# An attention-plus-experts block on one core: the list that orders every engine's work is planned anew

## The chip, the cores and the metric

The kernel runs on one core of a Trainium2 chip. The metric is the device time of one execution in microseconds (us), median of several runs; lower is better. Times below are counted from the start of the profiled span.

## The reference, cut to what matters

Two sequences of 2048 tokens with 128 features are normalised, then go through causal attention and through a layer of 8 experts; the results are added. Each token goes to the one expert whose centroid matches it best.

```python
def block(x, qk, ov, centroids, ln_g, ln_b, w1, b1, w2, b2):      # x: (2, 2048, 128)
    xn = layernorm(x)
    scores = einsum('bsd,de,bte->bst', xn, qk, xn) / sqrt(128)     # causal mask, softmax
    attn = einsum('bst,btd,de->bse', softmax(scores), xn, ov)
    eid = argmax(xn @ centroids.T)                                 # one of 8 experts
    alpha = sigmoid(sum(xn * centroids[eid]))
    xln = layernorm(xn) * ln_g[eid] + ln_b[eid]
    ffn = relu(xln @ w1[eid] + b1[eid]) @ w2[eid] + b2[eid]        # 128 -> 512 -> 128
    return x + attn + xn + alpha * ffn
```

## The kernel before

All five engines are programmed by hand, with semaphores between them. One list, ORDER (line 68), holds 1120 entries such as `T.3` or `P.17`. Every engine walks the whole list once, in its own program, and emits the instructions that it has for each entry. So the list alone fixes the order on each engine; where an entry stands against the entries of another engine has no meaning by itself. The waits are in the code of the entries. An engine executes in order: an instruction that waits holds up all that stands behind it on that engine.

The work has these stages. The 32 tiles of 128 tokens are in 8 groups of 4.

- **Normalising.** VAR (VectorE, statistics), LE (ScalarE, root), RN (GpSimd, one refining step on small columns), ROW (VectorE, line 799, groups 0, 1, 4, 6) or XA (ScalarE, line 1067, groups 2, 3, 5, 7).
- **Keys, queries, values, expert weights.** T, Q, V and W1 on TensorE; the entries with a, f or h (Ta, Qa, Vf, Va, W1h) copy the high half of a result out on ScalarE, those with l (Tl, Ql, Vl, W1l) the low half on VectorE, or on GpSimd for Vl.0, Vl.1 (line 741) and all W2l (line 735).
- **A first pass over the scores** for the row maxima: M (TensorE, line 1277), MR (VectorE, lines 892 and 896), RM, SH, SHa.
- **Attention** in 80 steps: X (scores, lines 1300 to 1304), EH and EX (exponential on ScalarE, lines 1044 and 1050), XL (VectorE, line 910, low half, from step 12), P and PB (weighted sums, lines 1334, 1343, 1344, 1351), QT (VectorE, lines 923 and 927, quotients).
- **Second normalising and routing.** R2 and R2n (VectorE) with R2a (ScalarE) make the second root; BASE and S (GpSimd, lines 641 and 651) add to and scale the rows; CH.0 and CH.1 (VectorE, lines 818 to 834) choose the expert of each half of the tokens; CNT (TensorE) and PL (VectorE, lines 849 to 860) work out each token's place; Sh and Sl make the two halves of a scaled row (Sl at line 1014); SIG makes the gate.
- **Sends.** 32 entries SC (GpSimd, line 684), one per tile, scatter the rows to an expert-sorted array in HBM, with a memset of 600 elements after each (line 671) to space them. SC.0 needs PL. Then SyncE reads the sorted rows back, transposed (line 526).
- **Experts.** 39 tiles: HI (TensorE, lines 1434 to 1436), RE (ScalarE, line 1166), LO (VectorE, line 1018), OUT (TensorE, lines 1456 to 1462), YS (ScalarE, line 1174), SO (GpSimd, line 693, scatter back). HI.0 needs all sends, since SyncE waits for them.
- **The rest of the attention** (steps 52 to 79) follows behind the experts on TensorE, then Y adds the experts' rows, and the results are stored.

GpSimd works in this order: the constants, RN, BASE, W2l, S, Vl.0 and Vl.1, then the 32 SC, W2l.5 to W2l.7, then the 39 SO. The part of CH that the prediction speaks of is three operations with both inputs in SBUF and four reductions:

```python
v.tensor_reduce(aff[:, on, :], parts, AX.X, ALU.add).then_inc(s_aff, 1)
v.wait_ge(s_aff, h + 1)
v.tensor_reduce(amax[:, on], aff[:, on, :], AX.X, ALU.max).then_inc(s_choose, 1)
v.wait_ge(s_choose, n + 1)
v.tensor_tensor(hit[:, on, :], aff[:, on, :], amax[:, on].unsqueeze(2).broadcast_to(wide),
                ALU.is_equal).then_inc(s_choose, 1)
```

Of the kernel before, what the change touches and what calls it, by code (L numbers as in the profile page):

```python
# [69 lines left out]
Vl.0 RN.3.4 BASE.2 RN.4.6 T.1 AE.1 AE.2 C1a LE.1.2 C2a Ta.0 W1h.0 W1h.1 Ta.1 W1l.0 Qa.0 Vf.0 LE.2.3 AE.3 W1l.1 AE.4  # L70
W1h.2 Va.0 Qa.1 LE.3.4 W1l.2 LE.4.6 XA.2 Vf.1 Ta.2 C2v C1v Tl.0 ROW.1.2 VAR.2.3 BASE.3 RN.6.8 W2l.0 W2l.1 BASE.4 BASE.5
BASE.6 BASE.7 W2l.2 Z.0 W2l.3 COL0 S.0 S.1 S.2 S.3 S.4 VAR.3.4 Tl.1 Ql.0 VAR.4.6 MR.0.0.0.0 Ql.1 MR.0.0.3.0 W1b.0 Q.0
V.0 W1.2 Z.1 Z.2 W1b.1 M.0.0.0.0 Q.1 MR.0.0.2.0 MR.0.0.1.0 VAR.6.8 RM.0.0 Tl.2 MR.0.1.1.0 M.0.0.3.0 S.5 S.6 W2l.4 W1.3
Z.3 S.7 W1b.2 M.0.0.1.0 M.0.0.2.0 V.1 T.2 M.0.1.1.0 W1.4 M.0.1.3.1 M.0.1.0.1 MR.0.1.3.1 MR.0.1.0.1 M.0.1.1.1 W1b.3
M.0.1.2.1 Q.2 M.0.1.3.0 MR.0.1.1.1 W1h.3 XA.3 LE.6.8 W1l.3 M.0.1.2.0 MR.0.1.2.1 MR.0.1.3.0 Ql.2 MR.0.1.2.0 SH.0.0
ROW.4.6 R2 ROW.6.8 MR.0.1.0.0 RM.0.1 MR.0.2.3.1 MR.0.2.1.1 MR.0.2.1.0 W1l.4 MR.0.2.3.2 MR.0.2.2.1 W1l.5 Qa.2 XA.5
SHa.0.0 AE.5 W2.0 W2.1 W1h.4 W1h.5 XA.7 EX.0 SHa.0.1 EX.1 W2.2 W2.3 M.0.2.3.1 M.0.2.1.1 M.0.1.0.0 W1.5 X.0 MR.0.2.2.0
R2a EX.2 EX.3 EX.4 Ta.3 Ta.4 Ta.5 W2.4 Ta.6 EX.5 Ta.7 Sh.0 Qa.3 EX.6 X.1 M.0.2.1.0 X.2 M.0.2.3.2 SH.0.1 M.0.2.2.1
M.0.2.1.2 X.3 M.0.2.2.0 M.0.2.0.1 P.0 M.0.2.0.0 X.4 M.0.2.0.2 MR.0.2.1.2 MR.0.2.0.1 M.0.2.3.0 P.1 T.3 T.4 T.5 X.5 P.2
T.6 P.3 T.7 X.6 M.0.2.2.2 MR.0.2.0.0 MR.0.2.0.2 MR.0.2.3.0 R2n Q.3 Tl.3 Tl.4 QT.0.0.0 Tl.5 Tl.6 QT.0.0.1 Tl.7  # L80
MR.0.2.2.2 Ql.3 RM.0.2 X.7 P.4 M.0.3.1.0 MR.0.3.1.0 M.0.3.3.1 MR.0.3.3.1 MR.0.3.2.0 M.0.3.2.0 X.8 AFF.0 AFFr.0.1
AFFr.0.2 M.0.3.1.1 X.9 AFFr.0.3 AFF.1 AFFr.1.1 X.10 P.5 MR.0.3.1.1 CH.0 Vl.1 MR.0.3.0.3 CH.1 Sl.0 SIG PL AFFr.1.2
M.0.3.0.3 P.6 AFFr.1.3 SH.0.2 M.0.3.3.2 X.11 V.2 P.7 CNT P.8 X.12 P.9 X.13 P.10 MR.0.3.3.2 Vl.2 QT.0.1.0 QT.0.1.1
# [25 lines left out]
YS.12 RE.29 RE.30 YS.13 RE.31 RE.32 YS.14 RE.33 YS.15 RE.34 RE.35 RE.36 YS.16 RE.37 XL.50 XL.51 QT.1.1.0 QT.1.1.1 LO.0
LO.1 M.1.3.3.0 X.51 PB.47 P.49 PB.48 P.50 PB.49 P.51 HI.0 PB.50 PB.51 HI.1 HI.2 OUT.0 LO.2 MR.1.3.1.0 MR.1.3.1.3 LO.3  # L110
OUT.1 HI.3 HI.4 OUT.2 HI.5 M.1.3.0.2 OUT.3 HI.6 OUT.4 HI.7 OUT.5 HI.8 OUT.6 LO.4 LO.5 LO.6 LO.7 LO.8 MR.1.3.0.2 LO.9
LO.10 LO.11 M.1.3.0.0 HI.9 OUT.7 HI.10 OUT.8 HI.11 OUT.9 HI.12 OUT.10 HI.13 OUT.11 HI.14 OUT.12 HI.15 OUT.13 HI.16
OUT.14 HI.17 LO.12 MR.1.3.3.0 LO.13 MR.1.3.0.0 LO.14 LO.15 LO.16 LO.17 MR.1.3.3.2 LO.18 MR.1.3.3.3 LO.19 LO.20 LO.21
LO.22 MR.1.3.0.3 LO.23 LO.24 LO.25 LO.26 LO.27 MR.1.3.1.2 LO.28 MR.1.3.2.0 LO.29 MR.1.3.2.1 LO.30 LO.31 LO.32
MR.1.3.2.2 LO.33 LO.34 OUT.15 M.1.3.3.2 HI.18 OUT.16 M.1.3.3.3 HI.19 OUT.17 M.1.3.0.3 SH.1.2 HI.20 OUT.18 HI.21 OUT.19
HI.22 OUT.20 HI.23 OUT.21 HI.24 OUT.22 HI.25 OUT.23 M.1.3.1.2 HI.26 M.1.3.2.1 OUT.24 HI.27 OUT.25 HI.28 M.1.3.2.0
OUT.26 HI.29 OUT.27 HI.30 OUT.28 M.1.3.2.2 HI.31 OUT.29 HI.32 OUT.30 M.1.3.2.3 HI.33 OUT.31 HI.34 OUT.32 MR.1.3.1.1
LO.35 LO.36 MR.1.3.3.1 LO.37 MR.1.3.2.3 LO.38 RM.1.3 XL.52 XL.53 HI.35 M.1.3.1.1 OUT.33 M.1.3.3.1 HI.36 OUT.34 HI.37
OUT.35 HI.38 OUT.36 X.52 OUT.37 X.53 X.54 P.52 X.55 PB.52 P.53 X.56 PB.53 P.54 X.57 PB.54 P.55 P.56 X.58 PB.55 SH.1.3
PB.56 X.59 P.57 PB.57 X.60 OUT.38 P.58 PB.58 P.59 X.61 X.62 PB.59 P.60 X.63 PB.60 X.64 P.61 P.62 PB.61 X.65 PB.62 P.63  # L120
X.66 P.64 X.67 PB.63 XL.54 XL.55 XL.56 XL.57 XL.58 XL.59 XL.60 XL.61 XL.62 XL.63 XL.64 XL.65 XL.66 XL.67 Y.6 XL.68 Y.0
XL.69 Y.7 XL.70 XL.71 Y.3 Y.2 Y.1 XL.72 Y.5 Y.4 XL.73 XL.74 QT.1.2.0 XL.75 XL.76 QT.1.2.1 XL.77 XL.78 XL.79 RE.38 EH.52
EX.52 YS.17 EH.53 EX.53 EH.54 EX.54 YS.18 EH.55 EX.55 EH.56 EX.56 EH.57 EX.57 EH.58 EX.58 EH.59 EX.59 SHa.1.3 EH.60
# [1372 lines left out]
```

## Time and profile before

| | us |
|---|---|
| three runs | 223.23, 223.56, 226.32 |
| their median | 223.56 |
| span of the profiled execution | 223.1 |
| TensorE busy in the span | 206.3 (92%) |
| VectorE busy | 175.5 (79%) |
| ScalarE busy | 155.2 (70%) |
| GpSimd busy | 154.3 (69%) |

The profile gives no time of its own for the profiled execution beside the span; the span lies 0.13 us below the fastest of the three runs and 0.46 us below their median. Reductions by 1 us are 0.45%. Engines in the rows: PE is TensorE, DVE is VectorE, ACT is ScalarE, POOL is GpSimd, SP is SyncE; L799 is line 799 of the kernel.

### The profile page before, as it was taken

The numbers are of one execution on the slowest core, as the hardware profiler recorded it, in microseconds if no ns is written. First come the engines' busy times: TensorE is split into PE (matmuls) and PEld (weight loads), VectorE is DVE, ScalarE is ACT, GpSimd is POOL, SyncE is SP. The second block draws the span as 40 slices with busy tenths as digits, with TensorE's granted clock in tenths as the row PEclk, the third lists the DMA queues.
The fourth block names the chain that finished last, engine by engine and source line by source line (L and its number), as shares of the span: only waits on it lengthen the run. The fifth ranks groups of instructions, "written<-read, shape, count | busy, mean of one in ns | idle before, by whom it ended". The sixth has DMA issues, their size and how long they took to land.

```text
span 223.1 us, 6878 instructions
## 1 busy us (share of the span) xinstructions
PE 206.3 (92%) x2428; PEld 159.9 (72%) x2428; DVE 175.5 (79%) x448; ACT 155.2 (70%) x346; POOL 154.3 (69%) x230
## 2 busy tenths in 40 slices
...
GB/s 167 314 289 64 6 0 94 116 355 232 5 12 39 36 39 39 44 43 40 36 40 36 128 198 160 125 92 141 131 150 92 50 40 37 38 35 172 256 193 141
DMA packets 37601, 23.55 MB, mean 106 GB/s; under 512 B 12472, under 2 KB 34144, under 8 KB 37568
## 3 DMA queue, kind: packets, MB, share of 16 engines
q1 hardware_dynamic: 34960, 18.28, 32.3%
...
q10 hardware_dynamic: 336, 0.14, 0.3%
q14 instruction: 13, 0.11, 0.2%
...
## 4 chain that ended last, share of the span: by engine, by line
PE 77%; DVE 11%; ACT 4%; issue 4%; DMA 2%; SPq 1%; DVEq 0%; ACTq 0%
PE psum L1343 6%; PE psum L1300 6%; PE psum L1301 6%; PE psum L1302 6%; PE psum L1351 6%; PE psum L1344 6%; PE psum L1277 5%; PE psum L1460 4%; PE psum L1461 4%; PE psum L1462 4%; PE psum L1434 4%; PE psum L1436 4%; PE psum L1435 4%; PE psum L1260 3%; PE psum L1334 2%
## 5 line engine op out<-in xcount | busy, mean ns | idle before, releaser
L910 DVE TENSOR_TENSOR p_lo<-p_sb,p_hi 128x512 f16<-128x512 f32 (+1 forms) x68 | 42.0, 638 | 12.2 <-ACT p_sb L1050 12.0
L1044 ACT ACTIVATE p_hi<-psum 128x512 f16<-128x512 f32 (+1 forms) x68 | 37.1, 547 | 19.4 <-PE psum L1351 14.2
L1050 ACT ACTIVATE p_sb<-psum 128x512 f32<-128x512 f32 (+1 forms) x80 | 42.5, 539 | 6.8 <-PE psum L1334 6.7
L693 POOL DMA_INDIRECT sorted_y<-xn x39 | 38.1, 977 | 11.6 <-ACT xn L1174 5.5
L1018 DVE SCALAR_TENSOR_TENSOR h_lo<-psum,h_hi 128x512 f16<-128x512 f32 x39 | 26.8, 690 | 21.5 <-ACT h_hi L1166 18.7
L671 POOL MEMSET v_full<- 1x600 f32 x71 | 41.7, 588 | 0.0
L684 POOL DMA_INDIRECT sorted_x<-xr,pos x32 | 33.5, 1047 | 11.9 <-issue 11.4
L1166 ACT ACTIVATE h_hi<-psum 128x512 f16<-128x512 f32 x39 | 23.3, 597 | 21.0 <-PE psum L1436 19.2
L1343 PE MATMUL psum<-v_hi,p_hi 128*128 128x129 f16 x236 | 32.7, 220 | 1.2 <-DVE x_sb L927 1.2
L896 DVE TENSOR_REDUCE row_max<-psum 128x1 f32<-128x512 f32 x48 | 32.3, 682 | 1.6 <-PE psum L1277 1.1
L1344 PE MATMUL psum<-v_lo,p_hi 128*128 128x128 f16 x236 | 32.6, 219 | 0.0
L1277 PE MATMUL psum<-kT_hi,qT_hi 128*128 128x512 f16 (+3 forms) x80 | 26.3, 349 | 4.5 <-DVE row_max L896 1.8
L1434 PE MATMUL psum<-x2T,w_hl 128*128 128x128 f16 x156 | 28.0, 219 | 0.2 <-issue 0.2
L1460 PE MATMUL psum<-w_hl,h_hi 128*128 x156 | 28.1, 219 | 0.0
L1461 PE MATMUL psum<-w_hl,h_hi 128*128 x156 | 28.1, 219 | 0.0
L1462 PE MATMUL psum<-w_hl,h_lo 128*128 x156 | 28.1, 219 | 0.0
L1436 PE MATMUL psum<-x2T,w_hl 128*128 128x128 f16 x156 | 28.0, 219 | 0.0
L1435 PE MATMUL psum<-x2T,w_hl 128*128 128x128 f16 x156 | 28.0, 219 | 0.0
L1300 PE MATMUL psum<-qT_hi,kT_hi 128*128 128x512 f16 (+1 forms) x80 | 27.8, 347 | 0.0
L1302 PE MATMUL psum<-qT_hi,kT_lo 128*128 128x512 f16 (+1 forms) x80 | 27.8, 347 | 0.0
L1301 PE MATMUL psum<-qT_lo,kT_hi 128*128 128x512 f16 (+1 forms) x80 | 27.8, 347 | 0.0
L1343 PEld LDWEIGHTS psum<-v_hi,p_hi 128*128 128x128 f16 x236 | 23.0, 98 | 4.1 <-DVE x_sb L927 1.3
...
## 6 DMA issues: line engine op xcount, KB each, us to landing
...
sorted_y<-xn POOLq DMA_INDIRECT x39
sorted_x<-xr,pos POOLq DMA_INDIRECT x32
```

Of the source, the lines that this page charges most:

```text
L671: pool.memset(idle, 0.0).then_inc(s_idle, 1)
L693: pool.indirect_dma_start(out=sorted_y[:, :], out_offset=bass.IndirectOffsetOnAxis(ap=tokens, axis=0), in_=xs[:, t % SLOTS, 0:P], in_offse ...
L910: v.tensor_tensor(p_lo[:, u, off:GW], p_sb[:, u, off:GW], p_hi[:, u, off:GW], ALU.subtract).then_inc(s_plo, 1)
L1044: a.activation(p_hi[:, u, off:GW], bank[SCORE[n % R]][:, off:GW], ACT.Exp, scale=SCALE).then_inc(s_exph, 1)
L1050: a.activation(p_sb[:, u, off:GW], bank[SCORE[n % R]][:, off:GW], ACT.Exp, scale=SCALE).then_inc(s_exp, 1)
L1277: mm(at[:, 0:w], qT_hi[:, q:q + P], kT_hi[:, k:k + w], start=True, stop=True).then_inc(s_mm, 1)
L1300: mm(at[:, off:GW], kT_hi[:, kk], qT_hi[:, q], start=True, stop=False)
L1301: mm(at[:, off:GW], kT_hi[:, kk], qT_lo[:, q], start=False, stop=False)
L1302: m = mm(at[:, off:GW], kT_lo[:, kk], qT_hi[:, q], start=False, stop=not diag)
L1343: mm(to[i], w, v_hi[:, kt, 0:P + 1], start=(j == 0 and i % 2 == 0), stop=False, skip_group_check=True)
L1344: mm(to[i][:, 0:P], w, v_lo[:, kt, :], start=False, stop=False, skip_group_check=True)
L1460: mm(to, h_hi[:, h, at], hi, start=False, stop=False, skip_group_check=True)
```

## The change

Only the text of ORDER differs: the same 1120 entries in another sequence, planned with durations of a trace. No instruction, buffer or wait rule is changed. Some of the list's 60 lines; the first shows how the start differs, the others how the sends (SC) are now spread among other engines' entries:

```diff
-VAR.0.1 VAR.1.2 BIASa LE.0.1 C0a AE.0 WU C0 C1 C2 T.0 W1.0 W1.1 BIAS RN.0.1 ROW.0.1 RN.1.2 MISC BASE.0 BASE.1 RN.2.3
...
-QT.0.2.1 MR.1.0.2.0 XL.25 Ql.5 RM.1.0 MR.1.1.1.0 Ql.6 XL.26 MR.1.1.2.0 MR.1.1.0.1 SC.0 SC.1 SC.2 SC.3 SC.4 SC.5 SC.6
...
+VAR.0.1 WU VAR.1.2 LE.0.1 C0 BIASa RN.0.1 ROW.0.1 C0a BIAS C1 C2v C1a C1v Tl.0 LE.1.2 C2a C2 T.0 W1.0 ROW.1.2 AE.0 Ta.0
...
+S.7 V.2 EX.14 MR.0.3.3.1 XL.13 P.11 PICK SC.0 EH.15 X.13 Sh.2 XL.14 MR.0.3.1.1 X.14 X.15 M.0.3.0.0 M.0.3.3.1 EX.15 X.16
...
```

On GpSimd, here is the stretch from the constants to the first send, as a piece of the difference (- before, + now). L735 is W2l, L641 is BASE, L651 is S, L741 is Vl.1, L684 the first SC.

```order
 L755 TENSOR_TENSOR x_sb<-x_sb,col 128x32
-L651 TENSOR_TENSOR xn<-xn,r 128x4x127 x7
+L641 TENSOR_TENSOR x_sb<-x_sb,xn 128x4x127
+L735 TENSOR_TENSOR w_hl<-w_raw,w_hl 128x512
+L651 TENSOR_TENSOR xn<-xn,r 128x4x127 x2
 L735 TENSOR_TENSOR w_hl<-w_raw,w_hl 128x512
 L651 TENSOR_TENSOR xn<-xn,r 128x4x127
+L641 TENSOR_TENSOR x_sb<-x_sb,xn 128x4x127
...
 L741 TENSOR_TENSOR v_lo<-v_full,v_hi 128x512
+L651 TENSOR_TENSOR xn<-xn,r 128x4x127 x3
 L684 DMA sorted_x<-xr,pos 4992x130
```

Before, seven S stood together, then W2l.4, the eighth S and Vl.1. Now the S are mixed with three W2l and one BASE, and Vl.1 stands ahead of the last three; in all S.0, S.1, W2l.2, S.2, BASE.7, S.3, W2l.3, S.4, W2l.4, Vl.1, S.5, S.6, S.7.

On VectorE, this is what stands ahead of CH.0 and in it, before. L896 is MR, L818 begins CH.0.

```order
L971 SCALAR_TENSOR_TENSOR qT_lo<-psum,qT_hi 128x512
L904 TENSOR_REDUCE max_col<-row_max 128x4
L896 TENSOR_REDUCE row_max<-psum 128x1 x4
L818 TENSOR_REDUCE aff<-psum 128x128
L820 TENSOR_REDUCE amax<-aff 128x16
L822 TENSOR_TENSOR hit<-aff,amax 128x128
```

And now, from the same L904 to the end of CH.0 and on to what follows CH.1:

```order
L904 TENSOR_REDUCE max_col<-row_max 128x4
L896 TENSOR_REDUCE row_max<-psum 128x1
L818 TENSOR_REDUCE aff<-psum 128x128
L820 TENSOR_REDUCE amax<-aff 128x16
L822 TENSOR_TENSOR hit<-aff,amax 128x128
...
L834 TENSOR_REDUCE onehot_group<-onehot 128x32
L872 TENSOR_SCALAR eneg<-eneg 128x32
```

Three MR have moved from ahead of CH.0 to behind it, and SIG (L872) stands directly behind CH.1, ahead of one MR and Sl.0.

## Rows read from the trace of the kernel before

**Rows 1.** The page: busy shares, and the group of MR (busy us, mean ns).

```profile
PE 206.3 (92%) x2428; PEld 159.9 (72%) x2428; DVE 175.5 (79%) x448; ACT 155.2 (70%) x346; POOL 154.3 (69%) x230
...
L896 DVE TENSOR_REDUCE row_max<-psum 128x1 f32<-128x512 f32 x48 | 32.3, 682 | 1.6 <-PE psum L1277 1.1
```

**Rows 2.** Busy time of each engine in four stretches.

```profile
core 0: us, PE busy (x) PEld busy (x) DVE busy (x) ACT busy (x) POOL busy (x), PEclk, DMA share, GB/s
0.00:30.00 30.00, 24.13 (x108) 13.03 (x108) 23.61 (x112) 19.27 (x53) 16.71 (x60) 0.89 0.56 156
30.00:62.70 32.70, 28.55 (x264) 20.88 (x265) 30.21 (x84) 24.50 (x54) 21.10 (x26) 1.00 0.41 137
62.70:126.20 63.50, 61.83 (x669) 44.43 (x667) 60.82 (x142) 49.19 (x104) 54.41 (x66) 1.00 0.14 42
126.20:219.70 93.50, 91.83 (x1390) 81.55 (x1390) 59.77 (x109) 62.23 (x138) 62.04 (x79) 1.00 0.52 123
```

**Rows 3.** Sends, transposed loads, experts, last matmul (start us, us, engine, line, operation).

```profile
63.67 1.21 POOL L684 DMA_INDIRECT sorted_x<-xr,pos  x1 [6.63 <-issue]
...
121.93 1.31 SPq L526 DMA_TRANSPOSE x2T<-sorted_x  x1
...
126.19 0.23 PE L1434 MATMUL psum<-x2T,w_hl 128*128 128x128 f16 x1 [0.21 <-issue]
...
219.45 0.23 PE L1351 MATMUL psum<-v_hi,p_lo 128*128 128x129 f16 x1
```

**Rows 4.** VectorE's waits: line, waited for, us in total, times, longest.

```profile
DVE b_hl L960 <- ACT b_hi L1096: 1.3, 1, 1.3
...
DVE G_lo L953 <- ACT cent_hl L1091: 1.0, 1, 1.0
```

**Rows 5.** VectorE and GpSimd, single instructions where both read SBUF; first one alone.

```profile
31.32 0.34 DVE L799 TENSOR_SCALAR xn<-x_sb,mv,r 128x127 f32<-128x127 f32 x1
...
12.78 1.51 DVE L799 TENSOR_SCALAR xn<-x_sb,mv,r 128x127 f32<-128x127 f32 x1
...
13.03 1.16 POOL L641 TENSOR_TENSOR x_sb<-x_sb,xn 128x508 f32<-128x508 f32 x1
...
33.43 1.26 DVE L799 TENSOR_SCALAR xn<-x_sb,mv,r 128x127 f32<-128x127 f32 x1
...
121.85 2.04 DVE L910 TENSOR_TENSOR p_lo<-p_sb,p_hi 128x512 f16<-128x512 f32 x1
...
121.08 1.15 POOL L735 TENSOR_TENSOR w_hl<-w_raw,w_hl 128x512 f16<-128x512 f32 x1
...
122.19 1.15 POOL L735 TENSOR_TENSOR w_hl<-w_raw,w_hl 128x512 f16<-128x512 f32 x1
```

**Rows 6.** GpSimd, scaling of the rows (S): first, two in the middle, last.

```profile
43.80 1.04 POOL L651 TENSOR_TENSOR xn<-xn,r 128x508 f32<-128x508 f32 x1 [0.35 <-DVE r L771]
...
48.78 2.03 POOL L651 TENSOR_TENSOR xn<-xn,r 128x508 f32<-128x508 f32 x2
...
51.88 1.03 POOL L651 TENSOR_TENSOR xn<-xn,r 128x508 f32<-128x508 f32 x1
```

**Rows 7.** VectorE: CH.0 (three), CH.1 (one), Sl.0, PL's first and last instruction.

```profile
52.92 0.42 DVE L818 TENSOR_REDUCE aff<-psum 128x128 f32<-128x256 f32 x1
...
53.70 0.29 DVE L822 TENSOR_TENSOR hit<-aff,amax 128x128 f32<-128x128 f32 x1
...
55.00 0.38 DVE L834 TENSOR_REDUCE onehot_group<-onehot 128x32 f16<-128x128 f16 x1
...
56.84 0.35 DVE L822 TENSOR_TENSOR hit<-aff,amax 128x128 f32<-128x128 f32 x1
...
58.49 0.68 DVE L1014 TENSOR_TENSOR xr<-xn,xr 128x512 f16<-128x512 f32 x1
...
59.77 0.16 DVE L849 TENSOR_SCALAR tiles_f<-psum 128x8 f32<-128x8 f32 x1
...
62.47 0.18 DVE L860 CAST pos<-posf 128x32 uint32<-128x32 f32 x1
```

More of the change, by code:

```diff
@@ L68 @@
 ORDER = entries("""
-VAR.0.1 VAR.1.2 BIASa LE.0.1 C0a AE.0 WU C0 C1 C2 T.0 W1.0 W1.1 BIAS RN.0.1 ROW.0.1 RN.1.2 MISC BASE.0 BASE.1 RN.2.3
[L70 to L83, printed above, removed]
@@ L109 @@
[L109 to L123, printed above, removed]
@@ new lines @@
+M.0.1.1.0 Vf.1 Z.0 W1.4 Ta.2 Tl.2 MR.0.1.2.1 MR.0.1.1.0 W1l.2 RN.4.6 LE.4.6 M.0.1.3.1 AE.5 MR.0.1.3.1 MR.0.1.0.0 W1h.3
+LE.6.8 W2.0 W1b.3 M.0.1.0.0 MR.0.1.2.0 MR.0.1.3.0 M.0.1.2.0 W1l.3 RN.6.8 MISC ROW.4.6 M.0.1.3.0 SH.0.0 W1l.4 W2l.0
+W1h.4 MR.0.1.1.1 BASE.3 W1.5 MR.0.1.0.1 R2 SHa.0.0 Ql.2 M.0.1.1.1 Q.2 M.0.1.0.1 W2.1 X.0 BASE.4 X.1 ROW.6.8 Qa.2 BASE.5
+RM.0.1 W1h.5 W1l.5 M.0.2.3.2 M.0.2.1.1 X.2 M.0.2.1.0 X.3 P.0 MR.0.2.3.2 M.0.2.2.0 COL0 MR.0.2.1.1 MR.0.2.1.0 MR.0.2.2.0
+EX.0 XA.3 MR.0.2.2.1 BASE.6 M.0.2.2.1 EX.1 MR.0.2.3.1 P.1 XA.5 M.0.2.3.1 SH.0.1 W2l.1 S.0 M.0.2.0.1 M.0.2.0.0
@@ new lines @@
+MR.0.2.0.1 XA.7 M.0.2.1.2 S.1 SHa.0.1 R2a X.4 W2l.2 MR.0.2.0.0 EX.2 W2.2 Ta.3 Ta.4 P.2 MR.0.2.1.2 S.2 R2n EX.3
+M.0.2.0.2 T.3 MR.0.2.0.2 T.4 QT.0.0.0 Tl.3 BASE.7 Tl.4 T.5 Tl.5 Ta.5 X.5 X.6 M.0.2.3.0 EX.4 S.3 P.3 EX.5 MR.0.2.3.0 T.6
+QT.0.0.1 Z.1 Ta.6 T.7 Tl.6 Ta.7 Q.3 Qa.3 X.7 EX.6 W2.3 M.0.2.2.2 Tl.7 Ql.3 P.4 M.0.3.1.0 W2.4 MR.0.2.2.2 Sh.0 AFF.0
+AFFr.0.1 AFFr.0.2 AFFr.0.3 W2l.3 EX.7 X.8 AFF.1 S.4 Va.1 AFFr.1.1 RM.0.2 EX.8 SGa EX.9 MR.0.3.1.0 W2l.4 CH.0 CH.1 Vl.1
+SIG EX.10 AFFr.1.2 SHa.0.2 AFFr.1.3 SH.0.2 M.0.3.2.0 P.5 MR.0.3.2.0 X.9 S.5 EH.12 P.6 Sl.0 X.10 EX.11 P.7 EX.12 S.6
@@ new lines @@
+X.11 CNT PL QT.0.1.0 MR.0.3.0.1 QT.0.1.1 P.8 XL.12 Vl.2 P.9 Va.2 X.12 EH.13 EX.13 M.0.3.0.1 P.10 EH.14 MR.0.3.0.0 Sh.1
+S.7 V.2 EX.14 MR.0.3.3.1 XL.13 P.11 PICK SC.0 EH.15 X.13 Sh.2 XL.14 MR.0.3.1.1 X.14 X.15 M.0.3.0.0 M.0.3.3.1 EX.15 X.16
+SC.1 P.12 EH.16 Sl.1 MR.0.3.3.2 EX.16 EH.17 M.0.3.1.1 PB.12 EX.17 P.13 M.0.3.3.2 Sh.3 M.0.3.0.2 P.14 EH.18 XL.15 P.15
+PB.13 SC.2 SC.3 X.17 EX.18 X.18 MR.0.3.0.2 EH.19 Va.3 M.0.3.1.3 MR.0.3.1.3 PB.14 P.16 X.19 SC.4 SC.5 XL.16 M.0.3.0.3
+MR.0.3.0.3 SC.6 PB.15 M.0.3.2.3 M.0.3.3.3 MR.0.3.2.3 XL.17 SC.7 X.20 MR.0.3.3.3 EX.19 M.0.3.3.0 PB.16 MR.0.3.3.0 V.3
```

75 lines of the change are left out of this document (45 added, 30 removed).

## The prediction

> **What bounds the kernel now.** I read the busy shares first. TensorE works for 206.3 of 223.1 us [rows 1]: no instruction goes away, so only its 16.8 us of idle time can be won. The table by stretches says where that lies [rows 2]. From 126.2 to 219.7 us TensorE is busy for 91.83 of 93.5 us, and from 62.7 to 126.2 for 61.83 of 63.5; after 219.7 come 3.4 us of quotients and stores. The idle time is in the first 62.7 us, where TensorE works for 52.7 us. Its clock is 0.89 of full there in the first 30 us and 1.00, that is 2.4 GHz, from then on.
>
> What TensorE waits for in that stretch is VectorE: from 30 to 62.7 us it is busy for 30.21 of 32.7 us. It works 23.61 + 30.21 = 53.8 us up to the end of PL, so 8.9 us are idle, 6.4 of them in the first 30 [rows 2]. Two of its waits can be named: 1.3 us in BIAS (L960) and 1.0 us at line 953 [rows 4].
>
> The end of PL sets what follows. PL ends at 62.47 + 0.18 = 62.65 us [rows 7], the first send starts 1.02 us later, at 63.67, the transposed loads can begin at 121.93, and the first expert matmul runs at 126.19 [rows 3]. From the first send that is 62.5 us. It is a chain of 32 sends and idle-memsets on GpSimd, none of which the change shortens. Beside it VectorE is busy for 60.82 and TensorE for 61.83 of 63.5 us [rows 2], so all three are close to full, and the start of the experts can't move by more than PL moves. From the first expert matmul to the end of the span 223.1 - 126.2 = 96.9 us pass, nearly all TensorE's own work. So what PL gains or loses is what the kernel gains or loses.
>
> **The change, part by part.** *Work ahead of PL.* The durations are those of the trace, taken along the new order. Three MR (MR.0.3.3.1, MR.0.3.1.1, MR.0.3.0.3) fall behind PL. Two are whole ones, 32.3 / 48 = 0.67 us by the group [rows 1]; less the small overlap of neighbours and with the short third, they are some 1.4 us. They aren't saved: they come later, in a stretch that VectorE doesn't bound alone.
>
> *Two holds go.* Line 799 takes 0.34 us when GpSimd is quiet, but 1.51 us at 12.78, when BASE.0 runs from 13.03 to 14.19, and 1.26 us at 33.43, beside a W2l [rows 5]. It ends with GpSimd's instruction: 1.17 + 0.92 = 2.1 us lost. In the new order BASE.0 stands behind a second RN, and the last ROW falls where GpSimd waits for XA.3, so I count both as gone. If they meet again, 2.1 us come back.
>
> *Idle time.* BIAS waits for a load and stands behind RN.0.1 and ROW.0.1 now: its 1.3 us are covered by them. Of the other waits I take 1.5 us as gone, since C1a goes ahead of the A_e copies on ScalarE and the first T, Q and XA are out about a microsecond sooner. The 1.0 us at line 953 stays, since C2a depends on the same chain as before. So 8.9 - 2.8 = 6.1 us remain. The bounds are 3.0 (the start, the first load and line 953 alone) and 8.9 (nothing won).
>
> *PL without anything new:* 53.8 - 1.4 - 2.1 + 6.1 = 56.4 us, with bounds of 53.3 and 59.2. That is 6.3 us sooner than 62.65, and would be the gain of the kernel.
>
> *The new collision.* I don't expect to see this gain, and the reason lies in the order on GpSimd. Before, S.0 starts at 43.80, right behind R2n; S runs at 2.03 / 2 = 1.0 us a piece, and S.7 ends at 51.88 + 1.03 = 52.91 [rows 6]. CH.0 starts at 52.92 [rows 7]: they just miss each other. Now R2n comes sooner by 0.6 us (less work ahead), 2.1 us (the holds) and 2.0 us (idle time): S.0 starts at 39.1. But three W2l, one BASE and Vl.1 are mixed in, at 1.15 us or so each [rows 5], about 1.12 by their pitch: the run takes 8 x 1.0 + 5 x 1.12 = 13.6 us and ends at 52.7. CH.0 comes in the midst of it. Backward from PL at 56.4: PL is 62.65 - 59.77 = 2.88, Sl.0 and SIG 59.77 - 58.49 = 1.28, one MR 0.6, CH.0 55.38 - 52.92 = 2.46, and CH.1 the same [rows 7]. So CH.0 starts at 46.7, and its first operation with two inputs in SBUF (L822, 53.70 - 52.92 = 0.78 us later) at 47.5, 5.2 us before the run ends.
>
> What does such an operation do there? The third case in the rows tells most: line 910 is asked for at 121.85, while W2l.5 runs (121.08 to 122.23). It takes 2.04 us, to 123.89, which is 0.55 us behind the end of W2l.6 (122.19 + 1.15 = 123.34) [rows 5]. A row of that size takes 0.68 us alone, as Sl.0 shows [rows 7]. So it was let in neither when W2l.5 ended nor while W2l.6 ran: the two followed one another without a gap. If a run of two holds VectorE to its end, I expect a run without gaps to do so too. For L822 itself the trace shows next to nothing: 0.35 instead of 0.29 us at 56.84, beside the last 0.2 us of Vl.1 [rows 7]. Its cost has the bounds 0 and 5.2 us; I take 5.2, by the nearest row.
>
> *Sum.* L822 ends at 52.7 + 0.3, the rest of CH.0 takes 1.4, CH.1 2.5, Sl.0 and SIG 1.3, the MR 0.6, PL 2.9: PL ends at 61.7, against 62.65. TensorE stands at CNT meanwhile, with all attention steps behind it, but catches up: after it the sends set the pace. Result: 223.1 - 0.95 = 222.15, say 222.2 us. This goes by the span of 223.1; the median of the runs is 223.56.
>
> *After the sends.* The same matmuls in another mixture. I set them at nothing: TensorE is full, and the attention left over covers the last OUT. At the very end step 79's scores come closer to their PB; a few tenths.
>
> The Trainium skill (SBUF — State Buffer, "Who interferes with whom") says that a VectorE instruction with two SBUF inputs contends with a GpSimd instruction that reads SBUF, and that whoever issues first has the shared ports for the whole instruction. The holds at 12.78 and 33.43 agree with that. Read to the letter, each hold would end with one GpSimd instruction; the row at 121.85 shows a hold over two. What the letter would give here is the second rival.
>
> **The rivals.**
> 1. *No hold for these operations.* CH works on 128 x 128 elements, a quarter of what line 910 reads, and the trace shows no long hold of one; or ScalarE is late for W2l.3 or Vl.1, and the gap lets CH through. Then PL ends at 56.4 and the kernel takes 223.1 - 6.25 = 216.9 us. Against it: line 799 is as small (127 columns) and was held twice.
> 2. *One hold, one GpSimd instruction.* The six operations of CH would each wait for one instruction of the run: the first to 48.2, then 49.3, 50.4; behind the reductions of both halves 52, 52.7, and the last is free. CH.1 ends at 54.0 instead of 51.6, PL at 58.8: 223.1 - 3.85 = 219.2 us.
> 3. *Slower: the experts stall.* By the order, the TensorE work between HI.k and OUT.k falls below 2.5 us for 15 of 39 tiles, instead of 3 (12 matmuls an HI, 13 an OUT, at some 0.055 us). In between, RE on ScalarE and LO on VectorE must be done. If a tile needs 2.5 us, because a YS or an MR gets ahead, and the 12 added tiles each lose 0.4 us, 4.8 us are lost where TensorE is the bound: with the forecast's PL, 222.2 + 4.8 = 227.0 us. It decides from 1 us of such stalls on, which eats up what PL gains. Against it: TensorE lost only 93.5 - 91.8 = 1.7 us there before [rows 2].
>
> **How the numbers follow.** Forecast (held to the end of the run) 0.55, own range 221.0 to 224.0; rival 1 0.20; rival 2 0.14; rival 3 0.11. The range reaches into rival 1 and towards rival 3: 216.8 to 225.0. About 2% is what a measurement of this kernel can tell, so faster means below 219.1 and slower above 228.0: faster takes rival 1 and most of half of rival 2 and a little of the forecast, 0.20 + 0.07 + 0.02 = 0.29; slower is the far part of rival 3, 0.04; the rest, 0.67, is within 2%.
>
> **What would show it.** In the changed profile: S.0 near 39 and S.7 ending near 52.7; L822 of CH.0 with a duration of several us, ending with S.7; PL's end at 61 to 62; the first send 1 us later; the first expert matmul 62 us behind it; 92 to 94 us of TensorE from there. L822 at 0.3 us near 47.5 makes the forecast wrong, and rival 1 right; six operations of about 1 us each speak for rival 2; a first send at 63 and an end beyond 224 with waits ahead of line 1456 for rival 3. If the holds at line 799 are still there, or S.0 starts after 42, my walk of the first 40 us failed.

## The result, and the profile after

| | before | after |
|---|---|---|
| median of 20 runs each, us | 224.25 | 222.31 |
| lowest and highest | 222.11 to 226.32 | 221.39 to 224.81 |
| span of the profiled execution | 223.1 | 220.4 |
| end of PL | 62.65 | 59.48 |
| first send | 63.67 | 60.51 |
| first expert matmul | 126.19 | 123.09 |
| end of the last matmul | 219.68 | 217.11 |

The ratio is 0.9938 with an interval of 0.9916 to 0.9960: 0.6% or 1.4 us faster, less than the 2% that counts as a change. (It is less than the 1.9 us between the medians because it leaves out four executions that took over 1.5% more than the fastest of their kernel.) The two profiled executions differ by more, 2.7 us. The changed kernel's profiled execution took 222.19 us for a span of 220.4, so some 1.8 us lie around a span. The forecast of 222.2 took the span of before (223.1) for its time, and is therefore a forecast of a span.

The busy shares of the changed kernel, and the granted clock in 40 slices of the span:

```profile
PE 203.7 (92%) x2428; PEld 159.9 (73%) x2428; DVE 178.0 (81%) x448; ACT 154.4 (70%) x346; POOL 156.0 (71%) x230
...
PEclk9999997999999999999999999999999999999999
```

TensorE's busy time fell by 2.6 us [rows 1] though its instructions are the same. The table by stretches (its columns as in [rows 2]), cut at the milestones of this execution, says where:

```profile
0.00:30.00 30.00, 24.01 (x127) 13.04 (x128) 27.04 (x124) 23.31 (x61) 17.71 (x64) 1.00 0.70 201
30.00:59.50 29.50, 25.03 (x244) 20.32 (x243) 27.15 (x68) 18.00 (x42) 20.35 (x21) 0.94 0.32 106
59.50:123.10 63.60, 62.23 (x671) 44.71 (x671) 62.11 (x143) 50.68 (x108) 53.95 (x66) 1.00 0.14 42
123.10:217.10 94.00, 92.46 (x1392) 81.79 (x1391) 60.65 (x111) 62.42 (x138) 63.97 (x79) 1.00 0.53 119
...
30.00:32.00 2.00, 0.97 (x10) 0.64 (x8) 2.00 (x5) 2.00 (x7) 1.73 (x2) 1.00 0.44 126
32.00:37.00 5.00, 4.54 (x22) 3.67 (x22) 3.75 (x8) 1.82 (x6) 4.79 (x7) 0.66 0.00 0
```

Two things are to be seen. In the first 30 us the clock is now whole, where it was 0.89 [rows 2]; it falls to the lower level, 1.2 GHz, between 32 and 37 instead, after a stretch in which TensorE was busy for 0.97 of 2 us. And VectorE does 27.0 us of work in the first 30 instead of 23.6, which is the gain of the front. Not all of it is the order's. e3_mixture below has the order of before on every engine up to R2, but ran at a mean clock of 0.991 instead of 0.985, and it reaches R2 (its first line here) 1.6 us sooner (the first row is the kernel before, the second e3_mixture):

```profile
32.34 0.18 DVE L804 TENSOR_TENSOR ve<-r 128x32 f32<-128x32 f32 x1
...
30.75 0.19 DVE L808 TENSOR_TENSOR ve<-r 128x32 f32<-128x32 f32 x1
```

So about half of the 3.2 us by which PL came sooner goes with the longer stretch at the lower clock in the profiled execution of before, and not with the order. Behind PL the two kernels take the same time, 63.6 and 94.0 us instead of 63.5 and 93.5 [rows 2].

TensorE's idle time up to its last matmul is 217.11 - 203.75 = 13.4 us, and it was 219.68 - 206.33 = 13.4 before. So between these two executions TensorE gained nothing in waits, and 2.6 us in the time of its matmuls. The clock accounts for some 1.6 us of that, by an estimate: a mean of 0.985 over 223.1 us against 0.992 over 220.4, of which the missing shares are 3.4 and 1.8 us. What makes the rest isn't shown. Its waits are others now:

```profile
engine line waited for: us in total, times, longest us
PE psum L1239 <- DVE onehot_group L834: 2.6, 1, 2.6
...
PE psum L1351 <- DVE p_lo L910: 1.3, 2, 1.1
```

L1239 is CNT, which needs the last operation of CH.1; the second row is PB.47, which needs XL.47. Neither wait stands in the list of before. The first has its cause here, in GpSimd's run (line by line) and VectorE's CH:

```profile
39.45 1.04 POOL L651 TENSOR_TENSOR xn<-xn,r 128x508 f32<-128x508 f32 x1 [2.44 <-DVE r L771]
...
47.19 1.04 POOL L651 TENSOR_TENSOR xn<-xn,r 128x508 f32<-128x508 f32 x1
48.19 1.21 POOL L735 TENSOR_TENSOR w_hl<-w_raw,w_hl 128x512 f16<-128x512 f32 x1
49.36 1.16 POOL L741 TENSOR_TENSOR v_lo<-v_full,v_hi 128x512 f16<-128x512 f32 x1
50.48 3.12 POOL L651 TENSOR_TENSOR xn<-xn,r 128x508 f32<-128x508 f32 x3
...
47.50 0.88 DVE L822 TENSOR_TENSOR hit<-aff,amax 128x128 f32<-128x128 f32 x1
48.41 1.13 DVE L825 TENSOR_TENSOR hit<-hit,rank_w 128x128 f32<-128x128 f32 x1
49.58 0.29 DVE L828 TENSOR_REDUCE posf<-hit 128x16 f32<-128x128 f32 x1
49.90 0.78 DVE L830 TENSOR_TENSOR onehot<-hit,posf 128x128 f16<-128x128 f32 x1
...
51.77 0.94 DVE L822 TENSOR_TENSOR hit<-aff,amax 128x128 f32<-128x128 f32 x1
52.75 1.01 DVE L825 TENSOR_TENSOR hit<-hit,rank_w 128x128 f32<-128x128 f32 x1
...
59.30 0.18 DVE L860 CAST pos<-posf 128x32 uint32<-128x32 f32 x1
```

S.0 starts at 39.45 and L822 at 47.50, as forecast (39.1 and 47.5), and the run ends at 53.60. But L822 takes 0.88 us and not 5.5: it ends 0.15 us behind the S that ran when it was asked for (47.19 + 1.04 = 48.23). L825 ends as far behind W2l.4, L830 behind Vl.1, and so on. Five of the six operations wait for one GpSimd instruction each, 0.6 + 0.8 + 0.5 + 0.65 + 0.7 = 3.3 us over their 0.29 [rows 7]; the reductions (L828) aren't held.

The second wait:

```profile
115.79 1.11 POOL L684 DMA_INDIRECT sorted_x<-xr,pos  x1 [0.17 <-issue]
116.89 0.59 POOL L671 MEMSET v_full<- 1x600 f32 x1
117.46 2.26 POOL L735 TENSOR_TENSOR w_hl<-w_raw,w_hl 128x512 f16<-128x512 f32 x2
...
116.66 3.61 DVE L910 TENSOR_TENSOR p_lo<-p_sb,p_hi 128x512 f16<-128x512 f32 x1
...
120.33 0.40 PE L1351 MATMUL psum<-v_hi,p_lo 128*128 128x129 f16 x4 [1.13 <-DVE p_lo L910]
```

XL.47 is asked for 0.24 us before the last send ends and finishes at 120.27, 0.55 us behind the second W2l. It is the operation that took 2.04 us before [rows 5], and here it is held through the end of the send, a memset and two W2l. So there are holds of two kinds, and the forecast had taken its size from the wrong one.

### The profile page after: what moved, and what is told of

Its sections match the earlier page's. It is cut to its first block, busy times and chain, and to the rows that moved or that the text cites. A ratio compares the mean times of both kernels' runs of the same rounds, so it can differ in the third digit from the quotient of the medians.

```text
span 220.4 us, 6878 instructions
## 1 busy us (share of the span) xinstructions
PE 203.7 (92%) x2428; PEld 159.9 (73%) x2428; DVE 178.0 (81%) x448; ACT 154.4 (70%) x346; POOL 156.0 (71%) x230
## 4 chain that ended last, share of the span: by engine, by line
PE 47%; DVE 14%; POOL 11%; DMA 6%; issue 5%; SPq 1%; ACT 0%; DVEq 0%; POOLq 0%
POOL sorted_y L693 7%; PE psum L1277 4%; POOL v_full L671 4%; DVE p_lo L910 4%; PE psum L1351 3%; PE psum L1343 3%; PE psum L1344 3%; PE psum L1301 3%; PE psum L1300 3%; PE psum L1302 3%; PE psum L1434 3%; DMA sorted_y<-xn 3%; PE psum L1436 3%; PE psum L1435 3%; DMA xn<-sorted_y 3%
## 5 line engine op out<-in xcount | busy, mean ns | idle before, releaser
L910 DVE TENSOR_TENSOR p_lo<-p_sb,p_hi 128x512 f16<-128x512 f32 (+1 forms) x68 | 43.7, 658 | 10.9 <-ACT p_sb L1050 10.7
L693 POOL DMA_INDIRECT sorted_y<-xn x39 | 40.0, 1026 | 10.7 <-issue 5.3
L1018 DVE SCALAR_TENSOR_TENSOR h_lo<-psum,h_hi 128x512 f16<-128x512 f32 x39 | 26.8, 690 | 21.8 <-ACT h_hi L1166 19.7
L684 POOL DMA_INDIRECT sorted_x<-xr,pos x32 | 33.0, 1033 | 12.2 <-ACT v_hi L1122 6.9
L896 DVE TENSOR_REDUCE row_max<-psum 128x1 f32<-128x512 f32 x48 | 32.0, 683 | 1.4 <-PE psum L1277 1.3
L1344 PEld LDWEIGHTS psum<-v_lo,p_hi 128*128 128x128 f16 x236 | 23.1, 98 | 3.1
```

What stands on the lines that cost most here:

```text
L693: pool.indirect_dma_start(out=sorted_y[:, :], out_offset=bass.IndirectOffsetOnAxis(ap=tokens, axis=0), in_=xs[:, t % SLOTS, 0:P], in_offse ...
L910: v.tensor_tensor(p_lo[:, u, off:GW], p_sb[:, u, off:GW], p_hi[:, u, off:GW], ALU.subtract).then_inc(s_plo, 1)
L1344: mm(to[i][:, 0:P], w, v_lo[:, kt, :], start=False, stop=False, skip_group_check=True)
```

## The experiments

Theory A: an operation of VectorE with two inputs in SBUF waits for one GpSimd instruction, CH's waits move the end of PL and TensorE's CNT, and these set the end. Theory B: the hold lasts to the end of a run without gaps (the forecast). Theory C: PL's date doesn't decide. The ratios are to the kernel before, run on the same chip; the changed kernel has 0.9938 (0.9916 to 0.9960).

**e4_ports: the hold by itself.** A program of its own:

```diff
+    ("WWWWW", ("red", "E512")),
+    ("SSSSS", ("red", "CH")),
...
+                    ins = pool.tensor_tensor(out=w2_hl[:, i + 1, :], in0=w2_raw[:], in1=w2_hl[:, 0, :], op=ALU.subtract)
```

> No attention and no experts: the input is copied to the output, and runs of 2 to 6 GpSimd operations without gaps (W: 128x512 f32 and f16 to f16, S: 128x508 f32 scaled in place) are set against single VectorE operations of 128, 256 and 512 columns, asked for some 0.7 us into the run. Theory A: each VectorE operation ends 0.1 to 0.55 us behind the end of the GpSimd instruction that ran when it was asked for, whatever its size. Theory B: each ends behind the last instruction of the run. A third outcome, by which both rows of the traces so far would hold: those of 128 columns are let in at the next boundary, and those of 512 columns only at the end of the run.

One case with W and one with S, and the same form alone (L92 is W, L95 is S, L116 the form of XL, L118 that of L822):

```profile
9.80 0.29 DVE L118 TENSOR_TENSOR hit<-aff,amax 128x128 f32<-128x128 f32 x1
...
10.79 6.04 POOL L92 TENSOR_TENSOR w_hl<-w_raw,w_hl 128x512 f16<-128x512 f32 x5
11.46 1.02 DVE L116 TENSOR_TENSOR p_lo<-p_sb,p_hi 128x512 f16<-128x512 f32 x1
...
48.63 5.06 POOL L95 TENSOR_TENSOR xn<-xn,r 128x508 f32<-128x508 f32 x5
49.29 0.53 DVE L118 TENSOR_TENSOR hit<-aff,amax 128x128 f32<-128x128 f32 x1
```

The W run goes on to 16.83, but XL's form is through at 12.48; in the S run L822's is through at 49.82. All sizes and mixtures did so: theory A, and the size of the operation is not what holds XL.47. GpSimd's next instruction is held in turn: the run of five W takes 6.04 us against 5.59 in the case with the smallest hold. Each case stands twice in the program, and the second time agrees within 0.02 us.

**e11_ports2: what precedes the run.** The same program with indirect stores and memsets ahead of the W.

```diff
+    ("WW", R + ("E512",)),
+    ("mWW", R + ("E512",)),
+    ("DmWW", R + ("E512",)),
+    ("DmWWWW", R + ("E512", "E512")),
```

> No attention and no experts: the input is copied to the output. An indirect store (D), a memset of 600 elements (m) and 2 or 4 operations of the form of W2l (W) follow one another on GpSimd; VectorE asks for an operation of the form of XL while D, m or the first W runs. Theory A alone: it is let in at once beside D and m, and behind the first W otherwise. If a preceding indirect store or memset makes the hold last over all W that follow, as at XL.47 in the kernels, it ends 0.55 us behind the last W in those cases, and in the case without D and m behind the first.

Three of the cases (L111 is W, L107 the memset, L100 the store, L137 XL's form):

```profile
13.68 0.59 POOL L107 MEMSET idle<- 1x600 f32 x1
14.24 2.25 POOL L111 TENSOR_TENSOR w_hl<-w_raw,w_hl 128x512 f16<-128x512 f32 x2
14.37 2.68 DVE L137 TENSOR_TENSOR p_lo<-p_sb,p_hi 128x512 f16<-128x512 f32 x1
...
21.47 1.11 POOL L100 DMA_INDIRECT sorted_x<-rows_out,pos  x1 [0.68 <-POOL tick L92]
21.55 0.69 DVE L137 TENSOR_TENSOR p_lo<-p_sb,p_hi 128x512 f16<-128x512 f32 x1
...
36.63 6.45 DVE L137 TENSOR_TENSOR p_lo<-p_sb,p_hi 128x512 f16<-128x512 f32 x2
37.49 0.59 POOL L107 MEMSET idle<- 1x600 f32 x1
38.06 4.47 POOL L111 TENSOR_TENSOR w_hl<-w_raw,w_hl 128x512 f16<-128x512 f32 x4
```

Two W alone let it in after the first (11.53 to 12.55), as in e4_ports; there GpSimd waits for the end of the short memset that opens the case. Two W directly behind a memset hold it to 17.05, 0.56 us behind the second; four W hold the second of two operations to 43.08, 0.55 behind the fourth. Beside the store it runs in 0.69, but asked for in the store's last 0.2 us, as XL.47 is, it is held through the memset and both W (26.94 to 30.54). So the rows of both kinds were right, and the long hold belongs to runs that follow a memset for whose end GpSimd doesn't wait, which is what W2l.5 and W2l.6 do behind the last send. The run of CH has no memset ahead of it. Why a memset does that, the runs don't tell.

The Trainium skill (SBUF — State Buffer, "Who interferes with whom") gives the ports to whoever issues first, for the whole instruction. CH in the changed kernel and e4_ports agree with that (0.88 and 0.53 us, each to some 0.15 us behind one instruction); e11_ports2 doesn't, with 2.68 us over two.

**e3_mixture: GpSimd's part of the change alone.** All other engines follow the list of before.

```diff
+            mixed = entries("S.0 S.1 W2l.2 S.2 BASE.7 S.3 W2l.3 S.4 W2l.4 Vl.1 S.5 S.6 S.7")
```

> The list of before, with GpSimd alone taking S.0 to S.7 in the mixture of the change (W2l.2, BASE.7, W2l.3, W2l.4 and Vl.1 among them); all else as before. The run then lasts from about 42 or 43.8 to 57, and CH.0 and CH.1 fall into it. Theory A: the operations with two inputs in SBUF take 0.8 to 1.1 us each instead of 0.3, CH.0 and CH.1 together 2.6 to 3.2 us more, PL ends at 65.2 to 65.8, the span is 225.7 to 226.3. Theory B: one operation takes 3.7 us, PL ends at 66.4, the span is 226.8. Theory C: span 223.

Median 224.86, ratio 1.0046 (1.0017 to 1.0075): 1.0 us slower, less than expected. CH.1 and Sl.0 in it (L829 is L825 of before, L1018 is Sl.0):

```profile
55.65 1.01 DVE L829 TENSOR_TENSOR hit<-hit,rank_w 128x128 f32<-128x128 f32 x1
...
58.03 1.12 DVE L1018 TENSOR_TENSOR xr<-xn,xr 128x512 f16<-128x512 f32 x1
```

Vl.1 waited 2.7 us for ScalarE, so GpSimd stood still beside CH.0, which was free. The holds sum to 1.6 us, against 2.6 to 3.2 expected; each is of kind A. PL ends at 62.63, as in the profile of before, only because this execution came to CH.0 sooner: from CH.0's start to the end of PL it takes 11.3 us (51.34 to 62.63) instead of 9.7 [rows 7]. So the change's mixture alone costs time.

**e1_order and e2_no_hold: the price of a hold.** Both move work out of GpSimd's run; e2_no_hold differs only in W2l.3 and W2l.4, which are memsets there, so it leaves out work.

```diff
-W2l.0 BASE.3 BASE.4 BASE.5 COL0 BASE.6 W2l.1 S.0 S.1 W2l.2 S.2 BASE.7 S.3 W2l.3 S.4 W2l.4 Vl.1 S.5 S.6 S.7
+W2l.0 W2l.1 BASE.3 BASE.4 BASE.5 COL0 BASE.6 W2l.2 BASE.7 Vl.1 S.0 S.1 S.2 S.3 S.4 S.5 S.6 S.7 W2l.3 W2l.4
```

> The changed list, with W2l.1, W2l.2, BASE.7 and Vl.1 moved ahead of S.0 on GpSimd (ScalarE's W2.2 and Va.1 earlier for that), S.0 to S.7 in one piece, W2l.3 and W2l.4 behind S.7, the clearing of rows Z.1 to Z.3 earlier. Theory A (each operation of CH waits for one GpSimd instruction, and the end of PL sets the end): S.7 ends at 47.8, two operations of CH.0 are held, by W2l.3 and W2l.4, CH.1 is free; PL ends at 57.7 instead of 59.5, the span is 218.6 instead of 220.4. Theory B (held to the end of a run without gaps): the first held operation goes to 50.1, PL ends at 57.9, nearly the same; the operations' own durations tell A from B. Theory C (the end of PL doesn't set the end): PL earlier, span still 220.4.

> As the run e1_order, but W2l.3 and W2l.4 are memsets: the low halves of w2 of experts 3 and 4 are left out (set to zero). Nothing on GpSimd reads SBUF against CH.0 and CH.1 any more but the last 0.3 us of S.7. Theory A and B: CH.0 and CH.1 take 2.5 us each, PL ends at 56.5, the first send is at 57.5, the span is 217.4: 3.0 us less than with the changed list. Theory C: 220.4. If memsets hold VectorE too, PL ends at 57.7 as in e1_order.

e1_order: median 222.52, ratio 0.9941 (0.9915 to 0.9968), span 220.6, PL at 59.76: no gain over the changed kernel. e2_no_hold: 220.87, 0.9867 (0.9824 to 0.9910), span 219.2, PL at 58.26. In e1_order two operations of CH.0 take 1.23 and 1.13 us, 1.8 us over their 0.29; in e2_no_hold none is held. It came to CH.0 0.3 us later, so PL came 1.50 us sooner, and the span is 1.4 us shorter: nearly one to one, against theory C. But e1_order lost 1.8 us ahead of S.0. There, R2 and two W2l:

```profile
27.73 0.28 POOL L634 TENSOR_SCALAR_AFFINE_SELECT ahead<-onesf 128x64 f32<-128x64 f32 x1
27.98 2.26 POOL L736 TENSOR_TENSOR w_hl<-w_raw,w_hl 128x512 f16<-128x512 f32 x2
...
28.44 1.85 DVE L805 TENSOR_TENSOR ve<-r 128x32 f32<-128x32 f32 x1
```

My own edit, W2l.1 behind W2l.0, made a new hold: an operation on 32 columns takes 1.85 us, to the end of both W2l, which follow GpSimd's constants (L634, a select) without a gap. Ql.2 stands behind it on VectorE, TensorE waited 2.3 us for that instead of 1.2. The clock fell from 34 to 37.5 us here, 1.4 us later than in the changed kernel and as long; in e2_no_hold, with the same order, it was low from 32 to 38.5.

**e6_wait: the holds away, with all work done.**

```diff
+                    if e in (3, 4):
+                        pool.wait_ge(s_onehot, e - 2)
```

> The list of e1_order, with two waits added on GpSimd: W2l.3 waits until the one-hot of CH.0 is done, W2l.4 until that of CH.1 is. All work is done. Theory A: the operations of CH take 0.3 us each, as in e2_no_hold; against e1_order PL is 1.8 us earlier, at 58.0 with the clock as it was there, and the span is 218.9. If the two W2l now hold Sl.0 or PL instead, PL ends at 58.6 to 59.5.

Median 221.27, ratio 0.9890 (0.9855 to 0.9926), span 219.5, PL at 58.95. All six operations of CH take 0.29 us, and TensorE doesn't wait for CNT. PL is 0.8 us sooner than in e1_order, and not 1.8: S.0 started 0.2 us later, behind a clock that stayed low until 39, and SIG was held once, by W2l.4 (a tensor_scalar of 32 columns in 0.94 us instead of 0.17).

**e5_clock and e7_both: TensorE's waits ahead of the clock's fall.**

```diff
-R2 SHa.0.0 Ql.2
+Ql.2 R2 SHa.0.0
...
-ROW.6.8 Qa.2 BASE.5 RM.0.1 W1h.5 W1l.5
+W1l.5 ROW.6.8 Qa.2 BASE.5 RM.0.1 W1h.5
```

> The changed list with two entries of VectorE earlier: Ql.2 ahead of R2, and W1l.5 ahead of ROW.6.8. TensorE waits for these two (1.2 and 1.5 us, at 28.6 and 31.0), and its clock is granted at half from 32.2 to 36.5, where VectorE then waits for scores (0.72 and 0.53 us). If the waits bring the clock down: no stretch at half there, R2n and S.0 1.3 us earlier (38.1), CH held as before, PL ends at 58.2, span 219.1. If VectorE sets the pace there anyway, or the clock falls all the same: PL 59.5, span 220.4.

> The edits of e5_clock and e6_wait together. Theory A, and a clock that stays up: PL ends at 56.7, span 217.6, 1.8 us less than e5_clock and 2.8 less than the changed list. If the clock falls at 32 to 37 all the same: PL 58.0, span 218.9, as e6_wait.

e5_clock: median 222.21, ratio 0.9922 (0.9883 to 0.9962), PL at 58.57, span 220.6. e7_both: 220.46, 0.9845 (0.9814 to 0.9876), PL at 58.12, span 218.8. e7_both came out as expected for a clock that falls all the same (58.0 and 218.9). The clock fell at 33 to 37 in both, so that these two waits bring it down isn't shown. e5_clock teaches something else: PL 0.9 us sooner than in the changed kernel, and the end no sooner. Two stretches of it:

```profile
50.00:54.00 4.00, 1.40 (x15) 1.20 (x12) 3.77 (x9) 0.81 (x4) 2.68 (x3) 1.00 0.84 300
54.00:58.00 4.00, 3.97 (x27) 3.85 (x28) 3.68 (x13) 0.53 (x2) 0.00 (x0) 0.57 0.00 0
```

TensorE waited 2.6 us for CNT as in the changed kernel, but here its clock was at 0.57 in the 4 us behind the wait. Three of its four runs have a mean clock of 0.985 and spans of 220.4 to 220.6, one 0.992 and 219.3: the second fall goes with 1.2 us. In the trace PL's gain is lost among the sends. The first starts 0.9 us sooner than in the changed kernel (59.59 against 60.51) and the last 0.5 later (116.28 against 115.79); single sends take 0.96 to 1.44 us. What ties that to the clock isn't shown.

**e8_mr: the three MR put back ahead of CH.0.**

```diff
-M.0.3.1.0 W2.4
+M.0.3.1.0 M.0.3.3.1 M.0.3.1.1 M.0.3.0.3 W2.4
...
-RM.0.2 EX.8 SGa EX.9 MR.0.3.1.0 W2l.4 CH.0
+RM.0.2 EX.8 SGa EX.9 MR.0.3.1.0 W2l.4 MR.0.3.3.1 MR.0.3.1.1 MR.0.3.0.3 CH.0
```

> The changed list with MR.0.3.3.1, MR.0.3.1.1 and MR.0.3.0.3 (and their matmuls M) back ahead of CH.0. By the term of the prediction alone (1.4 us of work ahead of PL) PL ends at 60.9, span 221.9. By theory A, CH.0 then starts 1.6 us later, further into the run of GpSimd, and is held for 2.0 us instead of 3.3: PL ends at 59.8, span 220.8.

Median 220.79, ratio 0.9873 (0.9834 to 0.9911), span 219.1: faster than the changed kernel, where the prediction's term alone said 1.4 us slower. In CH.0 and CH.1 (L826, L831 and L823 are L825, L830 and L822):

```profile
48.44 1.09 DVE L826 TENSOR_TENSOR hit<-hit,rank_w 128x128 f32<-128x128 f32 x1
...
49.89 0.69 DVE L831 TENSOR_TENSOR onehot<-hit,posf 128x128 f16<-128x128 f32 x1
...
51.67 0.95 DVE L823 TENSOR_TENSOR hit<-aff,amax 128x128 f32<-128x128 f32 x1
```

The holds sum to 1.9 us, as expected by theory A (2.0). PL came at 58.69, 1.1 us sooner than expected, and the clock was whole up to 47 us in this execution, so S.0 started 1.1 us sooner than in the changed kernel (38.34 against 39.45). TensorE has the matmuls M of these MR to do ahead of CNT, and it doesn't wait there any more. The last send starts no sooner (115.85 against 115.79), but TensorE is 1.2 us further at XL.47, which escapes the hold: the first expert matmul comes at 121.75 instead of 123.09. So moving these MR behind PL didn't pay. It left a hole in TensorE's work as long as CH was held; in e2_no_hold and e6_wait, where the MR stand behind PL too and CH is free, there is none. How much of the gain is the closed hole's and how much the sooner S.0's, this run doesn't separate.

**e9_w5: XL.47 set free.**

```diff
+                    if e == 5:
+                        pool.wait_ge(s_plo, 40)
```

> The changed list, with one wait added on GpSimd: W2l.5 waits until XL.51 is done, so that W2l.5 and W2l.6 don't run beside XL.47. In the changed kernel XL.47 takes 3.61 us (to 0.55 us behind the end of W2l.6), and TensorE idles 1.13 us at 119.2 behind it. If that wait is on the path: XL.47 takes 0.68 us, TensorE's wait goes, the first expert matmul comes at 122.6 instead of 123.1 (the transposed loads allow no earlier), the span is 219.3 to 219.9. If the sends hide it: XL.47 0.68 us, span 220.4. If the W2l now hold up the first OUT: over 220.4.

Median 221.32, ratio 0.9896 (0.9861 to 0.9932), span 219.3.

```profile
116.49 0.69 DVE L913 TENSOR_TENSOR p_lo<-p_sb,p_hi 128x512 f16<-128x512 f32 x1
...
PE psum L1459 <- POOL w_hl L738: 0.8, 1, 0.8
```

XL.47 takes 0.69 us, TensorE's wait is gone, and the span is 1.1 us shorter, although the first OUT (L1459) now waits 0.8 us for W2l.7. PL is at 59.32, as in the changed kernel: an end that moves with PL unmoved. The first expert matmul comes at 121.37, sooner than the 122.6 that I had taken for the limit of the loads; the first load is issued at 118.13. So what had set its time was the hold of XL.47, whose end hangs on the W2l behind the last send.

**e10_all and e12_best: what pays, together.**

```diff
-S.3 W2l.3 S.4 W2l.4 Vl.1 S.5 S.6 S.7
+S.3 S.4 S.5 S.6 S.7 W2l.3 W2l.4
...
+                    if e in (3, 4):
+                        pool.wait_ge(s_onehot, e - 2)
+                    if e == 5:
+                        pool.wait_ge(s_plo, 40)
```

> All together: the order of GpSimd and the two waits of e6_wait, the three MR ahead of CH.0 as in e8_mr, the wait of e9_w5. Theory A: CH.0 and CH.1 take 2.5 us each from about 47.3 on, PL ends at 57.0 (58.2 with a stretch at half clock ahead of 40), TensorE waits neither for CNT (2.6 us in the changed kernel) nor for XL.47 (1.1 us); the span is 216.8 to 217.9. If TensorE's work alone sets the end and its waits only move: 219 or more.

> What paid in the runs so far, without the early W2l.1 of e1_order (whose R2 was held for 1.85 us beside W2l.0 and W2l.1): the changed list, the three MR ahead of CH.0 as in e8_mr; Va.1 and Vl.1 ahead of S.0, S.4 to S.7 ahead of W2l.3, which waits for the one-hot of CH.0, and W2l.4 for that of CH.1; the wait of e9_w5; Z.2 and Z.3 ahead of W2l.3's load. All work is done. Theory A: of the operations of CH one is held by S.7 (some 0.4 us), against 1.9 us in e8_mr; PL ends at 57.4; TensorE waits neither for CNT nor for XL.47; the span is 217.0 to 217.9. If TensorE has no waits left that these edits take away: as e8_mr, 219.

e10_all, on the list of e1_order: median 222.44, ratio 0.9943 (0.9921 to 0.9965), PL at 60.76. A miss: it has the hold of R2 again (1.85 us), TensorE's waits of 2.3 and 2.0 us at 28 to 34, the clock low from 33 to 39.5, and three more MR behind all that. e12_best, without the early W2l.1 (the diff above; Vl.1 goes ahead of S.0): 220.90, 0.9855 (0.9808 to 0.9902), PL at 58.41, span 219.6. Both are over what was expected (57.4, and 217.0 to 217.9); SIG was held by W2l.4 in this order too, for 0.94 us. The first load, TensorE's longest wait, and the clock behind it:

```profile
118.08 1.31 SPq L527 DMA_TRANSPOSE x2T<-sorted_x  x1
...
121.43 0.23 PE L1439 MATMUL psum<-x2T,w_hl 128*128 128x128 f16 x1 [1.94 <-DMA x2T<-sorted_x]
...
122.00:126.00 4.00, 4.00 (x43) 3.73 (x41) 2.91 (x7) 1.79 (x3) 0.85 (x1) 0.57 0.83 176
```

With the holds away TensorE reaches the experts first (L1439 is the first HI) and waits 1.9 us for the transposed rows; then its clock fell. Now the sends alone are the bound. e7_both (0.9845) and e12_best beat both kernels, with all work done, if by less than 2%; against each other they can't be told apart.

## Why the prediction was right, and where it wasn't

The time and the direction came out: 222.31 us against 222.2, within 2%. That it came so near is luck: two errors of about 2 us cancel in that number. The span came to 220.4 instead of 222.15, and 1.8 us lie around a span.

- *Work ahead of PL, holds at line 799, idle time: the sum held, not all of its parts.* VectorE is busy for 54.2 us up to the end of PL; without the 3.3 us of CH and one hold at line 799 (30.38, 1.20 us beside BASE.3, so 0.9 us) that is 50.0, and the prediction had 53.8 - 1.4 - 2.1 = 50.3. Its idle time is 5.3 us instead of 6.1; the wait at line 953, which was to stay at 1.0 us, is 0.2. The walk to S.0 and L822 met both within 0.4 us. One hold that was counted as gone stayed, and R2 has a new one beside W2l.0 (0.74 us instead of 0.18). By e3_mixture about 1.6 us of what the order was to win goes with the clock, for which the sum had no term.
- *The new collision: seen in the right place, of the wrong size.* The step that failed is "If a run of two holds VectorE to its end, I expect a run without gaps to do so too." The row at 121.85 [rows 5] is a run that follows a memset; e11_ports2 shows that such a run holds to its end, and e4_ports that others let VectorE in at each boundary. The term was 5.2 us in one operation and measured 3.3 in five. Rival 2 described this mechanism; it gave PL at 58.8, and PL came at 59.5. The hold at 12.78 [rows 5], which the prediction reads as one of a single instruction, is not clearly that: line 799 was asked for 0.25 us ahead of BASE.0, while a select of GpSimd's constants ran (L633, 12.78 to 13.06).
- *"TensorE stands at CNT meanwhile ..., but catches up: after it the sends set the pace": held, but with a hold of its own behind the sends.* Starts in us, from the traces:

| | first send | last send | first expert matmul | behind the last send | end of span |
|---|---|---|---|---|---|
| before | 63.67 | 119.55 | 126.19 | 6.64 | 223.1 |
| changed | 60.51 | 115.79 | 123.09 | 7.30 | 220.4 |
| e6_wait | 59.97 | 115.26 | 122.55 | 7.29 | 219.5 |
| e5_clock | 59.59 | 116.28 | 123.57 | 7.29 | 220.6 |
| e8_mr | 59.70 | 115.85 | 121.75 | 5.90 | 219.1 |
| e9_w5 | 60.34 | 115.62 | 121.37 | 5.75 | 219.3 |
| e12_best | 59.43 | 115.64 | 121.43 | 5.79 | 219.6 |

In e12_best TensorE waits for the load, so 5.8 us are what the sends themselves need; the rest is XL.47's hold behind the W2l that follow the last send, with TensorE's work behind it. e6_wait has no wait at CNT and the same 7.29: the 2.6 us at CNT cost the end nothing beyond what they cost PL, which needs CNT as well. That "the start of the experts can't move by more than PL moves" is wrong by this hold: e9_w5 moved it by 1.7 us with PL 0.2 us sooner. "What PL gains or loses is what the kernel gains or loses" held from e1_order to e2_no_hold (1.50 and 1.4) and failed in e5_clock, where the sends took longer.
- *"I set them at nothing", after the sends: nearly.* From the first expert matmul to the end of the span it is 97.3 instead of 96.9 us. Rival 3 didn't come: TensorE idles 94.00 - 92.46 = 1.5 us in its experts and the rest, before 1.7 [rows 2].
- *Not in the sum: the clock.* The 2.7 us between the two profiles are 3.2 at the first send and 0.6 in the sends, less 0.7 in the hold behind them and 0.4 in the rest. By e3_mixture some 1.6 of the 3.2 go with the clock. Over all runs the gain is 1.4 us, and most of that remains where the clock is the same: at a mean of 0.992 the median span is 220.4 us in 14 executions of the changed kernel and 221.6 in 27 of the kernel before, on the chips of the other experiments.
